# The first layer's score strips move from the end of a cycle to the place between its maxima and its weighing

## The reference, cut to what matters

```python
x = x + _L0_xattn_ref(_layernorm(x), ctx, W, b)
x = x + _L0_attn_ref(_layernorm(x), Wq, bq, Wk, bk, Wv, bv, Wo, bo, slopes)
#   scores = einsum('bhqd,bhkd->bhqk', q, k) / sqrt(d) + slopes * dist     16 heads of 16, 64 x 64 positions
#   attn = softmax(scores); ctx = attn @ v; out = ctx @ Wo.T + bo
x = x + _L0_ffn_ref(...)      # routed and shared experts
x = x + _L1_xattn_ref(_layernorm(x), ctx, Wq, bq, Wk, bk, Wv, bv, Wo, bo)  # 16 heads, 64 queries x 1601 keys
x = x + _L1_attn_ref(...)     # convolution, gated recurrence, feed-forward
x = x + _L1_ffn_ref(...)      # quantised feed-forward
```

## Time and profile before

| what | value |
|---|---|
| median of 3 runs | 2220.2 us (2218.78 to 2221.45) |
| the profiled execution | 2225.24 us, its span 2223.3 us |
| granted clock, mean over the span | 0.973 |
| PE busy | 2024.7 us, 91% |
| DVE busy | 1353.2 us, 61% |
| ACT busy | 1092.5 us, 49% |
| POOL busy | 557.3 us, 25% |

### The profile page before, as it was taken

One profiled execution on the slowest core, in us unless ns is written; L12 is line 12 of the kernel. 1 busy time (PEld: TensorE's weight loads), 2 busy tenths in 40 slices (PEclk: granted clock), 3 DMA queues, 4 the chain that ended last, 5 costly groups with the idle time before them and its releaser, 6 DMA issues.

```text
span 2223.3 us, 73290 instructions
## 1 busy us (share of the span) xinstructions
PE 2024.7 (91%) x31814; PEld 1607.0 (72%) x31814; DVE 1353.2 (61%) x2525; ACT 1092.5 (49%) x2302; POOL 557.3 (25%) x966
## 2 busy tenths in 40 slices
PE   4788999899999999999999999999999988999977
PEld 4567777777878777777777778777777766777754
DVE  3456656755666666566666575675656566555543
ACT  2354555555455555445555544555544444444431
POOL 3122323222223131323223122322222222122201
PEclk8799999999999999999999999999999999999999
DMA  5343432343433333424232424143432302222121
GB/s 178 139 154 104 160 116 98 113 137 116 142 110 104 114 108 128 141 87 160 82 120 108 137 89 142 65 147 103 146 106 91 119 26 77 83 86 74 52 73 57
DMA packets 99116, 243.94 MB, mean 110 GB/s; under 512 B 13168, under 2 KB 19440, under 8 KB 98800
## 3 DMA queue, kind: packets, MB, share of 16 engines
q1 hardware_dynamic: 98800, 239.26, 31.8%
HBM read 235.94 MB, written 3.15 MB: 108 GB/s over the span
## 4 chain that ended last, share of the span: by engine, by line
PE 68%; DVE 14%; ACT 11%; issue 4%; SPq 1%; DMA 1%; POOL 1%; DVEq 0%; POOLq 0%; ACTq 0%
PE M L751 10%; PE M L758 9%; PE SC L930 9%; PE O L973 8%; PE SC L953 7%; ACT probT L1153 6%; DVE mx L1473 5%; PE X L780 4%; PE M L780 3%; PE SC L946 3%; PE X L1039 2%; PE M L821 2%; PE X L1027 1%; DVE V L1293 1%; ACT kT L1098 1%
## 5 line engine op out<-in xcount | busy, mean ns | idle before, releaser
L1473 DVE TENSOR_REDUCE mx<-SC 128x4 f32<-128x1600 f32 (+1 forms) x256 | 466.6, 1822 | 208.3 <-PE SC L930 204.6
L1153 ACT ACTIVATE probT<-SC 128x512 f32<-128x512 f32 (+1 forms) x1024 | 444.7, 522 | 168.0 <-PE SC L953 165.7
L1098 ACT ACTIVATE kT<-M,bk 128x400 f32<-128x400 f32 (+1 forms) x256 | 153.2, 598 | 536.4 <-PE M L751 536.0
L612 POOL TENSOR_TENSOR rowsT<-raw,rowsT 128x384 fp32r<-128x384 f32 (+1 forms) x256 | 280.7, 1117 | 403.5 <-ACT rowsT L1210 402.1
L758 PE MATMUL M<-wvs,rowsT 128*128 128x256 f32 x2496 | 361.2, 294 | 2.0 <-ACT kT L1098 1.6
L751 PE MATMUL M<-rowsT,wks 128*128 128x400 f32 (+1 forms) x1536 | 357.2, 368 | 3.5 <-POOL rowsT L612 2.3
L758 PEld LDWEIGHTS M<-wvs,rowsT 128*128 128x128 f32 x2496 | 316.3, 193 | 25.6 <-ACT kT L1098 2.0
L930 PE MATMUL SC<-kT,bdq 32*128 32x400 f32 (+1 forms) x2048 | 254.4, 566 | 71.7 <-ACT probT L1153 46.7
L751 PEld LDWEIGHTS M<-rowsT,wks 128*128 128x128 f32 x1536 | 271.9, 191 | 43.7 <-issue 22.3
L973 PEld LDWEIGHTS O<-probT,V 128*17 128x17 f32 x13312 | 197.2, 99 | 135.0 <-issue 120.2
L1293 DVE TENSOR_TENSOR V<-M,bv 128x256 f32<-128x256 f32 (+1 forms) x448 | 159.7, 398 | 205.9 <-PE M L758 197.5
(11 more groups left out here) (253 smaller groups left out, 2443.3 us busy)
## 6 DMA issues: line engine op xcount, KB each, us to landing
ring<-in_ws_dram SPq DMA_DIRECT2D x428, 256.0 KB, 4.6
raw<-in_ctx_dram SPq DMA_DIRECT2D x32, 1601.0 KB, 6.9
summed<-in_ctx_dram SPq DMA_DIRECT2D x60, 800.5 KB, 4.6
ring<-rounded_scratch SPq DMA_DIRECT2D x64, 256.0 KB, 6.0
out_dram<-x SPq DMA_DIRECT2D x16, 128.0 KB, 1.7
x<-in_x_dram SPq DMA_DIRECT2D x1, 1792.0 KB, 10.6
kT<-in_ctx_dram SPq DMA_DIRECT2D x2, 800.5 KB, 8.7
rounded_scratch<-wround SPq DMA_DIRECT2D x8, 128.0 KB, 2.1
```

The lines of the kernel that those rows point to most:

```text
L612: pool.tensor_tensor(rowsT[1][:, c, at], raw[:, c, at], rowsT[0][:, c, at], ALU.subtract).then_inc(low_ready, 1)
L1098: act.activation(keys(n, c)[:, k0:k0 + kn], bank[:, 0:kn], ACT.Identity, bias=bk[:, c:c + 1]).then_inc(m_used[f % 2], 1)
L1153: act.activation(probT[step % 2][0:w, j, 0:len(ts), :].rearrange("p t q -> p (t q)"), SC[0:w, j, 0:len(ts) * P], ACT.Exp)\
L1473: dve.tensor_reduce(mx[c][:, :, n], SC[:, :, 0:KCH[n][1]], AX.X, ALU.max).then_inc(max_used, 1)
```

## The change

The strips get a place of their own, "strips". On PE it lies directly behind maxima and, except for k = 0, ahead of weigh; before, they were the last pieces of "second". On ACT and DVE the place lies directly ahead of "second", behind the drains of place C. The numbers of the pieces, and with them the banks, follow the new order: the strips now come ahead of the cycle's key or value piece.

```diff
-        (4, "second"): ["l0_v"], (5, "second"): ["l0_s0", "l0_s1"], ...
+        (4, "second"): ["l0_v"], (5, "strips"): ["l0_s0", "l0_s1"], ...
@@ def pieces(b, k, half):
-    for what in (FIRST, SECOND)[half == "second"][k]:
+    for what in {"first": FIRST[k], "second": SECOND[k]}.get(half, ()):
@@ count_all
-        for what in pieces(b, k, "second"):
-            count(what, NUMBER, what[1], cycle)
+        for half in ("strips", "second"):
+            for what in pieces(b, k, half):
+                count(what, NUMBER, what[1], cycle)
@@ PE
                     maxima(b, k)
+                    for what in pieces(b, k, "strips"):
+                        fill(what)
                     if k not in WEIGH_FIRST:
                         weigh(*last(b, k))
@@ ACT and DVE
-                    for what in pieces(b, k, "second"):
-                        drain(what)
+                    for half in ("strips", "second"):
+                        for what in pieces(b, k, half):
+                            drain(what)
```

More of the change, by code:

```diff
@@ L71 @@
 L0_M = {(1, "second"): ["l0_turn1"], (2, "first"): ["l0_xa"], (3, "second"): ["l0_turn2"], (4, "first"): ["l0_qk"],
-        (4, "second"): ["l0_v"], (5, "second"): ["l0_s0", "l0_s1"], (8, "second"): ["l0_pt0"], (9, "first"): ["l0_pt1"],
+        (4, "second"): ["l0_v"], (5, "strips"): ["l0_s0", "l0_s1"], (8, "second"): ["l0_pt0"], (9, "first"): ["l0_pt1"],
         (9, "second"): ["l0_pv0"], (10, "first"): ["l0_pv1"], (10, "second"): ["l0_wo"], (12, "second"): ["l0_turn3"],
```

## The result

| | median us | runs | range us |
|---|---|---|---|
| before | 2221.93 | 20 | 2218.78 to 2226.43 |
| changed | 2217.59 | 20 | 2211.59 to 2225.45 |

The ratio is 0.9981, with a 95% interval from 0.9972 to 0.9989: about 4.2 us faster, with an interval of 2.4 to 6.2 us. The interval doesn't reach 1, so the gain is real, if just under the 0.2% (4.4 us) that the prediction drew between faster and no change. The forecast was 2219.0 us, in a range of 2216 to 2224.

A forecast was written before the change was run, and what follows sets the result against it. PE, busy 91% of the span, was taken as the bound. Waits 1.0 us lost and clock 1.8 gained made 0.8 faster: from 2220.2 to 2219.4, forecast as 2219.0 us, range 2216 to 2224 (8 in 10: 2208 to 2229).

The forecast's parts named there:

- The sum: Whole kernel: waits 1.0 us lost less clock 1.8 gained, so 0.8 us faster.
- Waits at k = 6: Four cycles where weigh covers the strips' add: waits of 0.78 go, 3.1 us gained, plus 1.2 at the scaled row.
- Waits at k = 2 and 3: Three cycles where place C delays DVE's strip adds: PE waits 3.7, 3.7 and 2.2 us; net 5.2 and 1.4 lost.
- rival (B): DVE's order at k = 2 and 3 makes PE wait, falls at k = 6 stay: slower, 2228 us; chance 0.21.
- k = 0, 4 and 1: Seven cycles: 0.2 us lost over three at k = 0, 1.0 gained over three at k = 4, 0.5 gained at k = 1.
- Sum of the waits: PE's waits over all moved strips: gains 5.8, losses 6.8, net 1.0 us lost; bounds 4 lost to 2 gained.
- The clock: PE's falls to 1.2 GHz behind the strips: net 1.8 us gained; bounds 15 gained to 10 lost.
- rival (A): Removing the wait before the strips removes most clock falls, none come at k = 4: faster, 2209 us; chance 0.33.
- (C): PE waits for the next cycle's exponentials instead, no gain or loss at k = 6: 2222 to 2224 us; chance 0.08.

The follow-up runs named there:

- second experiment: Kernel before, with the strips moved only in the three cycles with k = 2 or 3: 2228.43 us, 1.0039 of before.
- the third: Changed kernel, with DVE adding the strips directly behind its maxima, ahead of the copy of O and place C: 2204.26 us, 0.9936 of before.
- fourth: Kernel before, order unchanged, with three unused matmuls per cycle from the third tile on, put into the wait ahead of the strips: 2209.70 us, 0.9955 of before.
- eighth: Kernel before, with three unused matmuls in the same 14 cycles ahead of the key or value piece, the strips' wait left empty: 2227.48 us, 1.0032 of before.
- ninth: Kernel before, with strips moved only at k = 6 and three unused matmuls in the wait ahead of the ten other strips: 2205.08 us, 0.9929 of before.
- seventh experiment: Changed kernel, with 12 of the 16 strip matmuls left out in the last 14 tiles: 2211.25 us, 0.9968 of before.
- sixth experiment: Changed kernel, DVE adding strips behind its maxima; at k = 0 and 4 strips unmoved, three unused matmuls in their wait: 2196.59 us, 0.9903 of before.

## Why the prediction was right

The time, 2217.59, lies 1.4 us from the forecast of 2219.0, and part of that is luck. The sum had 0.8 us of gain and the forecast 1.2, from a base of 2220.2; the gain was 4.2 us, 3.5 to 5 times as much. The base was the median of three runs, and 20 runs gave 2221.93, which took back 1.7 us of the error. What held is the mechanism: waits gone at k = 6, new waits for the strips' adds at k = 2 and 3 of nearly the same size, and a small gain by the clock on top. The term that was mis-sized is the clock.

**Waits at k = 6.** Forecast: four times 0.78 gone and half of 2.3 us for the scaled row. The trace has them gone, and behind cycle 38 the wait of 1.29 became 0.37 and 0.30, of which the second is for the exponentials, as forecast:

```profile
414.17 0.44 PE L981 MATMUL X<-ident,rb 128*128 128x128 f32 x2 [0.37 <-ACT mT L1165]
...
414.91 0.95 PE L931 MATMUL SC<-kT,bdq 32*128 32x400 f32 x8 [0.30 <-ACT probT L1156]
```

**Waits at k = 2 and 3.** Forecast 3.7, 3.7 and 2.2; measured 3.32, 3.32 and 1.77. The working laid the strips' 2.3 us on top of maxima's end as the timeline gives it. In the trace the strips start 0.75 us behind maxima's start and not 0.88, and weigh 2.13 behind the strips' start (737.21 to 739.34). Both steps were a little shorter than counted. In cycle 51 DVE read the result of "out" at 518.93 where 519.1 was forecast, and PE was through with it at 518.89 where 518.7 was; so PE waited 1.77 and not 2.2:

```profile
516.90 1.99 PE L1011 MATMUL X<-ring,oT 128*128 128x256 f32 x8
...
520.66 1.36 PE L752 MATMUL M<-rowsT,wks 128*128 128x400 f32 x6 [1.77 <-DVE SA L1321]
```

The second experiment prices these waits with what hangs on them at 8.7 us, the third takes them away. The rival (B) was right in its mechanism and wrong in its weight: its condition, that the falls at k = 6 stay, did not hold.

**k = 0, 4 and 1.** Forecast a wait of 0.85 and measured 0.92 (k = 0). At k = 4 forecast 0.6 each; measured 0.69 in cycle 92 and 0.2 in the two others, with 0.57 left ahead of the strips in cycle 148. At k = 1, 0.32 stayed.

**Sum of the waits.** Forecast 1.0 us lost; PE's waits grew by 1.7 us between the profiled executions, and the runs leave between nothing and 2 us gained beside the clock. All three lie within some 4 us of each other, and the measurement doesn't decide the sign. The single waits above are surer than their sum.

**The clock.** Forecast net 1.8 us gained, from 19 of 23.9 us of falls gone at k = 6, 8.5 more at k = 4, and 3.4 more each at k = 2 and 3. The profile has 23.9 of 23.9 gone at k = 6, 10.2 more at k = 4, 3.4 more at k = 3, 3.4 less at k = 2 and 3.4 less at k = 0: net 17 us or 7.6 by the same price, in that one execution. But two profiles overstate it: the clock of the profiled execution before, 0.973, is low even for that kernel. By the mean clocks of all runs the clock gave 2 to 4 us. So the term was too small by a factor of one to two and a half. Three pieces went wrong in it. A fifth of the falls at k = 6 was let stay and all went; the k = 2 cycles were to fall for longer and in the profile fell for less; and a microsecond at the low clock was priced at 0.45 us, from the length of maxima, where the runs show 0.32. The first two made the gain too small and the third too large. The rival (A) had the falls at k = 6 right; its condition that none comes at k = 4 failed, with 10.2 us more there. The length of a wait did not decide either: cycle 106, with a wait of 3.32 us, fell for as long as before, and cycle 12, with one of 0.21, fell for 6.8 us where it had not fallen before. The cause assumed for it was tested: filling the wait removes most falls (fourth), the same work elsewhere doesn't (eighth), and a kernel with both the wait moved away and the others filled has hardly any (ninth). The mean clocks over all runs of these kernels, 0.9828, 0.9761 and 0.9850, bear this out. What exactly of the strips and the wait brings the clock down is not shown: the seventh experiment keeps its falls with a quarter of the strips, and also has more waits, and single falls came behind strips without any wait beside them (cycle 51 of the sixth experiment, cycle 78 of the ninth).

**(C), that the wait only moves,** is seen in small: waits for the exponentials grew from 46.7 to 49.5 us. It took back 2.8 of what went.

## What to carry to other kernels

Before a block of work is moved, find what the next user of its buffer waits for, in every variant of the cycle: here the same move was worth 8 us in one kind of cycle (k = 6) and cost 9 in another (k = 2 and 3), and the consumer's place on the other engine's list decided it. Moving the consumer too (the adds directly behind the reduction) gained a further 10 us on top of the 4 of the move itself. And read the granted clock behind each short wait: the waits of 0.78 us beside small matmuls (11.7 us in all) cost about their own length again in slower work, and matmuls without use, put into them, gave 10 us back. Where runs differ by how often the clock falls, compare the mean granted clock over all runs before a term is explained from two profiles.

## What the runs showed of the hardware

The clock fell to 1.2 GHz behind a stretch in which PE was busy for 2.56 of 3.40 us, and how often it fell was not the same in every execution of one program: the changed kernel's 20 runs spread over 13.9 us, 0.6%, with the mean granted clock between 0.974 and 0.980. Three runs of the kernel before lay within 2.7 us, and 20 of them within 7.7. Within one kernel, 0.001 of the mean clock went with 1.4 us. 42 matmuls whose results nobody reads made the kernel 10.0 us faster in one place and 7.1 us slower in another.
